# Part of the activations turned by VectorE in 32x32 blocks, a two-pass output product and a new order of the step, in a fused adapter FFN kernel

## The reference

```python
# layer 0: gated FFN with adapters on all three products, then a product with signs
gate = x @ Wg.T + 0.5 * (x @ Ag[id].T) @ Bg[id].T         # 512 -> 1376
up   = x @ Wu.T + 0.5 * (x @ Au[id].T) @ Bu[id].T
act  = silu(gate) * up
down = act @ Wd.T + 0.5 * (act @ Ad[id].T) @ Bd[id].T     # 1376 -> 512
x1   = x + down @ sign(W0).T + bias0
# layer 1: adapter pair alone, then a dense product with summed adapters
c    = (x1 @ B1[id1].T) @ A1[id1].T                       # rank 16
out  = x1 + c @ (W1 + 2 * sum_n w[n] * lB[n] @ lA[n]).T + bias1
```

## Time and profile before

| | |
|---|---|
| median of 3 runs | 1069.38 us (1067.91 to 1071.42) |
| profiled execution | 1067.19 us, span in the profile 1065.2 us |
| granted TensorE clock, mean | 0.991 |
| busy, share of the span | PE 97%, weight loads 87%, VectorE 50%, ScalarE 35%, GpSimd 24% |
| a step in the loop | 30.5 us, of 32 |

### The profile page before, as it was taken

How to read it: one execution, slowest core, us unless ns; L and a number is a source line. 1 busy time by engine, 2 the same in 40 slices (tenths; PEclk the granted TensorE clock), 3 DMA queues, 4 the chain that set the end, 5 groups by cost and what they waited for, 6 DMA issues and landing times.

```text
span 1065.2 us, 18157 instructions
## 1 busy us (share of the span) xinstructions
PE 1035.6 (97%) x5940; PEld 923.3 (87%) x5940; DVE 532.5 (50%) x992; ACT 378.1 (35%) x668; POOL 255.4 (24%) x362
## 2 busy tenths in 40 slices
PE   5979999999999999999999999999999999999996
PEld 4858888999988888999888889998889899989894
DVE  5574544454555444555554544555545445555443
ACT  3762333333333332333333323333333233333321
POOL 1012122222221222222212222221222222212311
PEclk9999999999999999999999999999999999999998
DMA  8923133332322333323233333232233332223311
GB/s 298 351 90 77 51 99 91 97 99 83 89 60 76 99 89 99 99 80 87 62 78 99 89 99 99 76 87 61 82 99 89 99 98 77 85 60 87 99 40 40
DMA packets 66058, 101.75 MB, mean 96 GB/s; under 512 B 25264, under 2 KB 41648, under 8 KB 65536
## 3 DMA queue, kind: packets, MB, share of 16 engines
q1 hardware_dynamic: 55008, 65.63, 20.4%
q0 software_dynamic: 11040, 36.00, 12.2%
HBM read 90.58 MB, written 11.01 MB: 95 GB/s over the span
## 4 chain that ended last, share of the span: by engine, by line
PE 96%; DVE 2%; DMA 1%; ACT 0%; issue 0%; POOL 0%; SPq 0%; DVEq 0%; ACTq 0%
PE gu_ps L823 54%; PE y_ps L898 26%; PE actT_ps L885 4%; PE x1T_ps L823 3%; PE y_ps L823 2%; PE mix_ps L823 1%; PE y_ps L915 1%; PE x1T_ps L923 1%; PE actT_ps L823 1%; DMA weff_raw<-in_w1T 1%; PE mix_ps L874 1%; DVE wu_sb L581 0%; PE mix_ps L908 0%; DMA x_sb<-in_x 0%; DVE b_sb L581 0%; DMA out_x<-x_sb 0%
## 5 line engine op out<-in xcount | busy, mean ns | idle before, releaser
L898 PE MATMUL y_ps<-down_sb,actT_sb 128*128 128x288 f32 (+1 forms) x2112 | 300.8, 297 | 0.7 <-DVE actT_sb L581 0.7
L898 PEld LDWEIGHTS y_ps<-down_sb,actT_sb 128*128 128x128 f32 (+1 forms) x2112 | 283.5, 188 | 1.2 <-DVE actT_sb L581 1.1
L823 PE MATMUL gu_ps<-wg_sb,xT_sb 128*128 128x512 f32 (+1 forms) x1152 | 278.7, 390 | 0.0
L823 PE MATMUL gu_ps<-wu_sb,xT_sb 128*128 128x512 f32 (+1 forms) x1152 | 257.7, 372 | 0.5 <-DVE wu_sb L581 0.5
L823 PEld LDWEIGHTS gu_ps<-wg_sb,xT_sb 128*128 128x128 f32 x1152 | 214.0, 189 | 40.9
L823 PEld LDWEIGHTS gu_ps<-wu_sb,xT_sb 128*128 128x128 f32 x1152 | 203.3, 188 | 31.1 <-DVE wu_sb L581 0.9
L353 POOL TENSOR_TENSOR x_sb<-x_sb,bias_sb 128x512 f32<-128x512 f32 x32 | 41.6, 1299 | 384.2 <-PE x1T_ps L923 384.2
L581 DVE TENSOR_TENSOR b_sb<-b_raw,b_sb 64x1024 fp32r<-64x1024 f32 (+2 forms) x128 | 120.4, 940 | 25.9 <-ACT b_sb L392 24.9
L436 ACT ACTIVATE act_sb<-gu_ps 128x512 f32<-128x512 f32 (+1 forms) x96 | 53.5, 557 | 181.2 <-PE gu_ps L823 181.2
L317 POOL DMA_INDIRECT b_raw<-in_btab,now x96 | 88.7, 924 | 81.5 <-POOL now L341 26.0
L581 DVE TENSOR_TENSOR actT_sb<-actT_ps,actT_sb 128x512 fp32r<-128x512 f32 (+1 forms) x96 | 62.1, 647 | 91.8 <-ACT actT_sb L392 91.8
(11 more groups left out here) (143 smaller groups left out, 922.1 us busy)
## 6 DMA issues: line engine op xcount, KB each, us to landing
a_raw<-in_atab SPq DMA_DIRECT2D x128, 152.0 KB, 2.3
xT_raw<-in_xT SPq DMA_DIRECT2D x32, 256.0 KB
x_sb<-in_x SPq DMA_DIRECT2D x32, 256.0 KB
out_x<-x_sb SPq DMA_DIRECT2D x32, 256.0 KB
b_raw<-in_b1tab SPq DMA_DIRECT2D x128, 32.0 KB
wd_raw<-in_wd SPq DMA_DIRECT2D x4, 688.0 KB, 10.6
wg_raw<-in_wgu SPq DMA_DIRECT2D x4, 688.0 KB, 6.0
wu_raw<-in_wgu SPq DMA_DIRECT2D x4, 688.0 KB, 9.5
```

What stands on the lines that cost most here:

```text
L823: last = nc.tensor.matmul(o, w, m, start=start and n == 0, stop=stop and n == len(terms) - 1, skip_group_check=not check)
L898: last = nc.tensor.matmul(y_ps[half][:, 0:MH], actT_sb[0:m, ACTT_SLOT[c] + n, a, :], down_sb[0:m, blk, b, half * MH:(half + 1) * MH], star ...
```

## The change

It has these parts:

- The second and third chunk are no longer transposed by TensorE. VectorE's new `turn` does it with 16 instructions per chunk, each of four 32x32 blocks (32 partitions by 128 elements), from `act_sb` into `actT_raw` in SBUF. `split_actT` reads that. The first chunk stays on TensorE.
- `turn(g, 2)` is cut in two: the first half is put before `add_out(prev)` at the end of a step, the second at the start of the next, and `split_actT(prev, 2)` moves to the start of the next step on both engines.
- `out_product` has two matmuls where it had three. The c rows are gathered for 64 partitions, and their low part is put into the other 64 (`c_sb` 128x512); `t1_sum` holds the same values in both halves, and `own_t1` makes it in five operations where it had three.
- `down(prev, 2)` moves behind `gate(g, 1)` and `lora(g, 0, ...)`.
- `split_xT`'s low part moves from VectorE to GpSimd. `split_b(g, 1)` and `split_b(g, 2)` move over the border into the step that uses them, `split_b1` into the next step; `split_sbd` and `split_c` move ahead of `gated(g, 1)`. GpSimd gathers sbd and c first, then adds bias0, and then gathers the next B rows.

```diff
+            def turn(g, c, quads, last):
+                if 0 in quads:
+                    dve.wait_ge(L["act_done"], g * NC + c + 1)
+                a = act_sb[:, ACT_SLOT[c], :].rearrange("p (n f) -> p n f", n=4)
+                for q in quads:
+                    for r in range(4):
+                        op = nc.vector.transpose(actT_raw[r * QUAD:(r + 1) * QUAD, :, q * QUAD:(q + 1) * QUAD],
+                                                 a[q * QUAD:(q + 1) * QUAD, :, r * QUAD:(r + 1) * QUAD])
+                if last:
+                    op.then_inc(L["turned"], 1)
...
             def own_t1(g):
                 dve.wait_ge(L["t1_mm"], g + 1)
-                nc.vector.tensor_copy(t1_sum[:], t1_ps[:, 0:P]).then_inc(L["t1_added"], 1)
-                dve.wait_ge(L["t1_added"], 2 * g + 1)
-                nc.vector.tensor_tensor(t1_sum[:], t1_sum[:], t1_ps[:, P:2 * P], ALU.add).then_inc(L["t1_added"], 1)
-                dve.wait_ge(L["t1_added"], 2 * g + 2)
-                nc.vector.tensor_tensor(t1_sum[:], t1_sum[:], own_row, ALU.mult).then_inc(L["t1_masked"], 1)
+                nc.vector.tensor_copy(t1_part[:], t1_ps[0:GR, 0:P]).then_inc(L["t1_added"], 1)
+                dve.wait_ge(L["t1_added"], 3 * g + 1)
+                nc.vector.tensor_tensor(t1_part[:], t1_part[:], t1_ps[0:GR, P:2 * P], ALU.add).then_inc(L["t1_added"], 1)
+                dve.wait_ge(L["t1_added"], 3 * g + 2)
+                nc.vector.tensor_tensor(t1_part[:], t1_part[:], t1_ps[GR:P, 0:P], ALU.add).then_inc(L["t1_added"], 1)
+                dve.wait_ge(L["t1_added"], 3 * g + 3)
+                for d in range(2):
+                    last = nc.vector.tensor_tensor(t1_sum[d * GR:(d + 1) * GR, :], t1_part[:], own_row[0:GR, :], ALU.mult)
+                last.then_inc(L["t1_masked"], 1)
...
-                product(out_ps[:], [(t1_sb[:, a, :], c_sb[:, b, :]) for a, b in THREE], L["out_mm"])
+                product(out_ps[:], [(t1_sb[:, a, :], c_sb[:]) for a in range(2)], L["out_mm"])
```

More of the change, by code:

```diff
@@ L699, in step @@
             def step(g, prev, nxt):
+                if prev is not None:
+                    turn(prev, 2, (2, 3), True)
                 if g is not None:
                     own_t(g)
+                if prev is not None:
+                    split_actT(prev, 2)
+                if g is not None:
                     split_t(g)
-                if prev is not None:
-                    own_td(prev)
-                if g is not None:
+                    split_b(g, 1)
+                    split_b(g, 2)
                     gated(g, 0)
@@ L708, in step @@
                 if prev is not None:
+                    split_b1(prev)
+                    own_td(prev)
                     split_td(prev)
@@ L713, in step @@
                     split_b(nxt, 0)
+                if g is not None:
+                    split_sbd(g)
+                if prev is not None:
+                    split_c(prev)
+                if g is not None:
+                    gated(g, 1)
                 if prev is not None:
@@ L716, in step @@
                 if g is not None:
-                    gated(g, 1)
-                    split_sbd(g)
-                    split_actT(g, 1)
+                    turn(g, 1, range(4), True)
                 if prev is not None:
                     split_x1(prev)
-                    split_c(prev)
+                if g is not None:
+                    split_actT(g, 1)
                 if nxt is not None:
-                    split_b(nxt, 1)
+                    split_a(nxt)
                 if g is not None:
@@ L728, in step @@
                     own_t1(prev)
-                if nxt is not None:
-                    split_a(nxt)
-                if prev is not None:
                     split_t1(prev)
-                if nxt is not None:
-                    split_xT(nxt)
                 if g is not None:
-                    split_b1(g)
-                if nxt is not None:
-                    split_b(nxt, 2)
-                if g is not None:
-                    split_actT(g, 2)
+                    turn(g, 2, (0, 1), False)
                 if prev is not None:
```

153 lines of the change are left out of this document (82 added, 71 removed).

## The result

The changed kernel takes 1148.89 us (median of 4 runs, 1148.52 to 1151.01) where the kernel before takes 1068.64 beside it: the ratio is 1.075, 95% interval 1.0726 to 1.0775. Slower, as forecast (1155 us). The profiled execution has a span of 1146.7 us, so 81.5 more than before.

A forecast was written before the change was run, and what follows sets the result against it. TensorE, busy 30.50 of a 30.5 us step, was taken as the bound; 3.88 us of waits less 1.05 of work make 33.33 us a step, with the ends +86 on 1067.2, so 1155 us, range 1135 to 1180.

The forecast's parts named there:

- the wait at td: TensorE before td_transpose: own_td stands behind the ad and b1 splits; 2.54 us against 0.72 of cover, 1.9 with refill.
- the 1.05 us of work that went: TensorE work leaving each step: second chunk's transposes 0.44 us, third's 0.35, one output-product matmul 0.26.
- The price of a transpose: VectorE block transposes, 32 a step: 0.32 us start to start, 5.12 for 16; bounds 0.20 and 0.45.
- The wait at x1: TensorE at x1_transpose: sbd and c splits ahead of gated and add_y; 3.74 us against 3.25 of cover, 0.5 wait.
- The wait at t: TensorE at t_transpose: own_t behind both half turns and add_out on VectorE, 16.29 against 14.95; 1.35 us wait.
- the gap at the output product: TensorE's output product, behind own_t1's five links and split_t1, ready at 9.77, waits until 9.90: 0.13 us.
- Step 0: First step: 0.8 us of transposes go and the stop before t_transpose shrinks, together -4 (from -2.5 to -5).
- Tail: After the last step: down(prev,2) waits 6.75 us behind the output product; add_y would have been ready 1.4 earlier; +4.6.
- Slower transposes: Rival, VectorE transposes at 0.36 to 0.45 us each: 1190 us at 0.36, 1280 at 0.45; chance 0.16.
- the overlap of transposes: Rival, VectorE transposes 0.20 us each, waits at t and output product go, td's and x1's stay: 1107 us; chance 0.14.
- The lower clock in each step: Rival, TensorE's clock drops after idle stretches, half speed over 6 us of each step: 1248 us; chance 0.05.
- The rival on the other side: Faster: td_masked in time, x1's about the only wait left if transposes are cheap too: 1046 us; chance 0.04.

The follow-up runs named there:

- the first experiment: The changed kernel with own_td(prev) on VectorE ahead of split_ad(g) and split_b1(prev): 1089.09 us, ratio 1.019 to the kernel before.
- The second experiment: The changed kernel with every block transpose writing to the 32 partitions it reads from (output not the reference's): 1110.65 us, ratio 1.0397 to the kernel before.
- the best of them: The changed kernel with own_td, gated and add_y, own_t and split_t moved ahead in VectorE's and ScalarE's queues: 1046.31 us, ratio 0.9785 to the kernel before.

## Why the prediction was right

**The sign and the wait at td.** Forecast 1.9 us a step from a sum of seven terms; measured 1.89, and the first experiment took out 59.8 us, 31 steps of 1.93. It is three quarters of the loss, but it does not decide the sign alone, and the last sentence of the prediction (no wait at td would break the sign) is wrong: with this wait gone the kernel still took 1089.09 us, 1.9% more than before, since the waits at x1 and t, 1.4 us a step, are more than the 1.05 us of work that went. Nothing of it could be seen in the profile of before, where own_td was ahead of split_ad: it came out of reading, for the moved block, what each engine's queue does between its last matmul and the next thing that TensorE wants.

**The price of a transpose.** Forecast 0.32 us start to start, from a neighbouring operation's length and from the row in which the output's partitions change; measured 0.316. The second experiment shows that the change of partitions is the cause of more than a third of it: where they stay the distance is 0.19. The Trainium skill (VectorE: DVE Perf Modes, "Two Vector instructions with no wait between them") says that an instruction whose first input or output starts in another group of 32 partitions than the last one's starts only when all earlier Vector instructions have finished; it states no price. Both traces agree: such a transpose starts 0.01 us behind the end of the one ahead, the others 0.06 before it.

**The wait at x1.** Forecast 0.5, measured 0.50.

**The wait at t** is the term that was mis-sized: forecast 1.35, measured 0.93. VectorE needed 598.26 + 0.49 - 582.82 = 15.9 us from x1_done to the end of own_t where the sum said 16.24 (half of that is in the first turn, which began 0.08 before x1_done and took 5.07 to the next start, not 5.15), and the gap at the output product (0.13 forecast) is only spread out: output product and gate(g,0) take 0.62 and 2.70 us instead of 0.52 and 2.61. So a step is 33.05 us instead of the 33.33 forecast. The sum of 86 us on the profiled execution came out as 81.6: 78.7 instead of 86.4 in the 31 steps, 2.2 in the prologue, which the sum had put at nothing and which differs as much between runs of any order, and 0.9 more in the two ends.

**The ends.** Step 0: forecast -4.8, measured -4.7. The stop before t_transpose is 3.13 us instead of 6.03, and the granted clock (72 to 78 us, the stop and what is behind it) is 1.00 where before it was 0.50 behind the stop. That this fits so well is partly luck: all ten kernels with this part of the change have a stop of 3.08 to 3.13 us here, and the granted clock behind it is 1.00 in four of the profiled executions and 0.50 for some 3 to 6 us in the other six. Tail: forecast +4.6, measured +5.4. There TensorE stops for 5.83 us, and the down block behind takes 5.09 us instead of 3.46, at a granted clock of 0.50 from 1128.4 to 1132 us; the sum had left that out:

```profile
1128.44 5.09 PE L929 MATMUL y_ps<-down_sb,actT_sb 128*128 128x288 f32 x24 [5.83 <-DVE actT_sb L601]
```

**The rivals.** Slower transposes and the overlap of transposes are both refuted by 0.316, and the kernel in which they do overlap came to 1111, where the rival had said 1107. The lower clock in each step did not come: the stretch of a whole step has 1.00, with stops of 1.66 us in it. The rival on the other side needed td_masked in time and hardly any other wait; it is what the later kernels do by order, and the estimate of 1046 us that went with it is, by chance of its terms, what the best of them takes.

What stays open: the best order is 29.71 us a step and not 29.45, and its trace has 0.22 us of the difference at lora(g,1,0), behind gated(g,0); whether that goes with faster splits of b was not tried. Nor was it tried to turn the first chunk on VectorE too (VectorE has 3 to 4 us of a step left).

## What to carry to other kernels

When work moves off a full engine, the gain is a small sum (here 1.05 us a step) and any wait is paid in full, so for every moved block walk the in-order queues of all engines between its last instruction and the next one that the full engine needs; an unrelated instruction that waits for the same signal, put ahead of the urgent one, cost 60 of the 80 us. Mend the orders one at a time but judge them together: moves that gave nothing in the kernel after were most of a gain of 16 us once the later wait was gone. Small VectorE instructions that change their partitions each time don't overlap; a transpose of 32x128 cost 0.316 us so, and 0.19 where the partitions stayed.

## What the runs showed of the hardware that was not expected

VectorE's low split of 64x1024, with two SBUF inputs, took 1.23 us in the mean before and 1.70 in the kernel after, up to 2.37 us where it met GpSimd's 128x512 addition; with that addition cut to one column it took 1.22. In the step shown the two splits take 3.45 us together instead of 2.47. A timeline of either engine alone does not show why.

A stop of TensorE of 3.1 us, the same in ten kernels, left the granted clock at 1.00 in four profiled executions and at 0.50, the lower of its two levels, in six. One profile does not tell what such a stop costs.
